# A fused cross-attention block: the read stage's sums moved to TensorE and its steps interleaved with the next block's

## The chip, the cores and the metric

One core of a Trainium2 chip. The metric is the device time of the whole kernel in microseconds, here the median of three runs of the same program; a profiled execution of its own gives the trace. Five engines work side by side and meet only through semaphores: TensorE (PE, matmuls; its weight loads are PEld), VectorE (DVE), ScalarE (ACT), GpSimd (POOL) and SyncE (SP), which here issues most DMAs.

## The reference

Two sequences of 1024 tokens with 2048 features each (512 features x 4 channels). What matters here is the first part:

```
x  = layernorm(x)                                  # over all 2048
y  = einsum('blhc,hoc->bloh', x, W)                # channel sums: 4 channels to 1, for o = Q, K, V
yn = (y - mean(y)) * rsqrt(var(y) + eps) * gamma + beta     # over 512 features, per output
q, k, v = yn[o] @ qkv_w[o].T                       # three 512 x 512 projections
q, k = rope(q), rope(k)
```

After it come causal attention with 16 heads of 32, a gated state write, a second read with two outputs, a large product with the context, a second write, a layer norm and a product with a 2048 x 2048 matrix of signs. None of these is touched.

## The kernel before

Features stand on the partitions and tokens along the free dimension. The work is cut into blocks of T = 512 tokens (NB = 4). Each stage is one function with one instruction list per engine, which its engine runs strictly in order; the order is written out by hand and the waits are semaphore waits.

`setup_phase` (lines 68 to 191) loads the projection weights and constants on SP's queue, and the first two blocks of x on POOL's (line 96), splits the weights into a high and a low part, and makes the rope tables. Its end is a barrier of all engines.

`read_phase` (lines 194 to 517) is the stage changed. X has shape [128, 2 halves, 16 feature tiles, 512]: tile c*4 + a holds channel c of features a*128 to a*128+127. For each block:

- Mean of x: 16 fp32 matmuls with a full 128x128 matrix of 1/2048 (`x_mean`, line 278), so that the sum stands on all partitions; one VectorE pass centres the block (line 428); ScalarE squares it in four pieces (364); 16 more matmuls (`x_var`, 287); ScalarE makes rstd by Ln and Exp (368, 370); one VectorE pass scales (433).
- Channel sums, on VectorE (`read`, 448 and 450): for each output and each of four 128-feature groups one multiplication and three multiply-adds over 512 elements.
- Per output: mean of y (`y_mean`, 301, 4 fp32 matmuls), centring (459), squares, variance (`y_var`, 311), scaling (463), and the affine with gamma and beta on VectorE (466). ScalarE makes ZH, a rounded copy (395), VectorE ZL, the rest (474).
- `project` (327): for each 128-token tile 12 matmuls (ZH x high, ZL x high, ZH x low, for four feature groups) into one PSUM bank, 48 per output. VectorE applies rope to Q and K tiles (486 to 492), ScalarE copies V tiles (415), SP stores them.

The order on PE within a block is: y_mean of all three outputs, with the next block's x_mean between them; y_var of all three; projection of output 0; the next block's x_var; projections of outputs 1 and 2. On VectorE: all channel sums, all centring, x_centre of the next block, scaling, rope of output 0, x_scale of the next block, rope of output 1. There is one ZH and one ZL, so each projection ends before the next output's ZH is made. X of block n+2 is loaded when block n's channel sums are done (249). The normalised x is stored by SP (259) and read again two stages later.

Of the kernel before, what the change touches and what calls it, by code (L numbers as in the profile page):

```python
# [5 lines left out]
F32 = mybir.dt.float32  # L6
# [6 lines left out]
P = 128  # L13
# [52 lines left out]

def setup_phase(nc, io, t):

    with ExitStack() as ctx:
        def ev(name, **k):  # L70
# [10 lines left out]
        idf = t["ident"]  # L81
# [7 lines left out]
                 (idf[:], io["ident"]), (t["masks"][:], io["masks"]), (t["read1"][:], io["read1"]),  # L89
                 (t["read1_gb"][:], io["read1_gb"])]  # L90
        with nc.Block() as block:
            @block.gpsimd
            def _(eng):
                eng.wait_ge(w_loaded.sem, w_loaded.at())
                for half in range(2):
                    eng.dma_start(t["X"][:, half], io["x"][:, :, half * T:(half + 1) * T]).then_inc(t["x_in"][half].sem, t["x_in"][half].unit)
# [10 lines left out]
            def _(eng):  # L107
# [56 lines left out]
                eng.wait_ge(dve_order.sem, dve_order.next(0))  # L164
                eng.wait_ge(w_loaded.sem, w_loaded.at())
# [5 lines left out]
            def _(eng):  # L171
# [18 lines left out]
                eng.activation(t["masks_r"][:], t["masks"][:], ACT.Copy).then_inc(act_order.sem, 1)  # L190
# [3 lines left out]
def read_phase(nc, io, t):  # L194

    with ExitStack() as ctx:
# [7 lines left out]
        SQ = sb("SQ", [P, 2, HC, T])  # L206
# [4 lines left out]
        RT = sb("RT", [P, 2, H])  # L211
        OUT = sb("OUT", [P, TT, H])
        ps = ctx.enter_context(nc.psum_tensor("ps1", [P, 8, 512], F32))
        MEAN, VAR, YM, YV, PJ = 0, 1, (2, 3, 1), (2, 3, 2), 4

        x_in = t["x_in"]
        xn_out = [ev(f"xn_out{a}", unit=16) for a in range(2)]
        mean, cent, xn, rsx = ev("mean"), ev("cent"), ev("xn"), ev("rsx")

        sq, sq_used = ev("sq", per=7, credit=4), ev("sq_used", per=7, credit=4)  # L220
        y, rs = ev("y", per=3), ev("rs", per=3)
        ym, yc, z, zh, zl = (ev(n, per=3) for n in ("ym", "yc", "z", "zh", "zl"))
        pj = ev("pj", per=3 * TT, credit=1)
        pjq_used = ev("pjq_used", per=2 * TT)
        pjv_used = ev("pjv_used", per=TT, credit=TT)
        qk_ready = ev("qk_ready", per=2 * TT)
        stored = [ev(f"stored{tt}", per=3, unit=16, credit=16) for tt in range(TT)]
        assert L // T == 2

        def blocks(eng, body):  # L230

            with eng.Fori(0, B - 1) as b:
                for half in range(2):
                    body(b * 2 + half, half, b, True)
            for half in range(2):
                body(NB - 2 + half, half, B - 1, half == 0)

        def slot(half, k):

            return (half + k + 1) % 2  # L240

        with nc.Block() as block:
            @block.gpsimd
            def _(eng):
                with eng.Fori(0, B - 1) as b:
                    for half in range(2):
                        eng.wait_ge(xn_out[half].sem, xn_out[half].at(b))
                        eng.wait_ge(y.sem, y.at(b * 2 + half, 3))
                        eng.dma_start(X[:, half], io["x"][:, :, bass.ds((b * 2 + half + 2) * T, T)]).then_inc(x_in[half].sem, x_in[half].unit)

            @block.sync
            def _(eng):
                for tt in range(TT):
                    eng.sem_inc(stored[tt].sem, 16)
                with eng.Fori(0, B) as b:
                    for half in range(2):
                        i = b * 2 + half
                        eng.wait_ge(xn.sem, xn.at(i))
                        eng.dma_start(io["xn"][:, :, bass.ds(i * T, T)], X[:, half]).then_inc(xn_out[half].sem, xn_out[half].unit)
                        for o in range(3):  # L260
                            for tt in range(TT):
                                if o < 2:
                                    eng.wait_ge(qk_ready.sem, qk_ready.at(i, o * TT + tt + 1))
                                else:
                                    eng.wait_ge(pjv_used.sem, pjv_used.at(i, tt + 1))
                                eng.dma_start(
                                    io["qkv_s"][:, o, bass.ds(b * (NH // 2), NH // 2), half * TT + tt:half * TT + tt + 1, :],
                                    OUT[:, tt].rearrange("p (h a d) -> p h a d", h=NH // 2, a=1)).then_inc(stored[tt].sem, stored[tt].unit)
                for half in range(2):
                    eng.wait_ge(xn_out[half].sem, xn_out[half].at(B - 1))  # L270
                for tt in range(TT):
                    eng.wait_ge(stored[tt].sem, stored[tt].at(NB - 1, 3))

            @block.tensor
            def _(eng):
                def x_mean(half, first, last):
                    for f in range(first, last):
                        mm = eng.matmul(ps[:, MEAN], t["ones_d"][:], X[:, half, f], start=f == 0, stop=f == NF - 1,
                                        skip_group_check=True)
                    return mm  # L280

                def x_var(i, k0, slot_of):

                    for g in range(4):
                        eng.wait_ge(sq.sem, sq.at(i, k0 + g + 1))
                        for f in range(HC):
                            mm = eng.matmul(ps[:, VAR], t["ones_d"][:], SQ[:, slot_of(g), f],
                                            start=g + f == 0, stop=g + f == 6)
                        mm.then_inc(sq_used.sem, sq_used.unit)

                eng.wait_ge(x_in[0].sem, x_in[0].at())
                x_mean(0, 0, NF).then_inc(mean.sem, mean.unit)
                x_var(0, -4, lambda g: g % 2)

                def body(i, half, b, more):
                    def y_mean(o):
                        eng.wait_ge(y.sem, y.at(i, o + 1))
                        if o == 2:
                            eng.wait_ge(rsx.sem, rsx.at(i))
                        for hc in range(HC):  # L300
                            mm = eng.matmul(ps[:, YM[o]], t["ones_h"][:], Y[:, o, hc], start=hc == 0, stop=hc == HC - 1,
                                            skip_group_check=True)
                        mm.then_inc(ym.sem, ym.unit)

                    def y_var(o):
                        eng.wait_ge(sq.sem, sq.at(i, o + 1))
                        eng.wait_ge(yc.sem, yc.at(i, o + 1))
                        if o == 2:
                            eng.wait_ge(rs.sem, rs.at(i, 1))
                        for hc in range(HC):  # L310
                            mm = eng.matmul(ps[:, YV[o]], t["ones_h"][:], SQ[:, slot(half, o + 1), hc],
                                            start=hc == 0, stop=hc == HC - 1)
                        mm.then_inc(sq_used.sem, sq_used.unit)

                    def project(o):
                        eng.wait_ge(zh.sem, zh.at(i, o + 1))
                        eng.wait_ge(zl.sem, zl.at(i, o + 1))
                        for tt in range(TT):
                            n = o * TT + tt
                            if o == 0:  # L320
                                eng.wait_ge(pjv_used.sem, pjv_used.at(i, n + 1 - TT))
                            else:
                                eng.wait_ge(pjq_used.sem, pjq_used.at(i, n + 1 - TT))
                            step = 0
                            for ic in range(HC):
                                for zz, ww in ((ZH, "qkv_h"), (ZL, "qkv_h"), (ZH, "qkv_l")):
                                    mm = eng.matmul(ps[:, PJ + tt], zz[:, ic, tt * P:(tt + 1) * P],  # L327
                                                    t[ww][:, bass.ts(o * HC + ic, H)],
                                                    start=step == 0, stop=step == 3 * HC - 1)
                                    step += 1  # L330
                            mm.then_inc(pj.sem, pj.unit)

                    y_mean(0)
                    if more:
                        eng.wait_ge(x_in[1 - half].sem, x_in[1 - half].at(b + half))
                        eng.wait_ge(cent.sem, cent.at(i))
                        x_mean(1 - half, 0, NF // 2)
                    y_mean(1)
                    if more:
                        x_mean(1 - half, NF // 2, NF).then_inc(mean.sem, mean.unit)  # L340
                    y_mean(2)
# [1694 lines left out]
```

## Time and profile before

| | us |
|---|---|
| median of three runs | 2495.5 (2489.01 to 2499.91) |
| profiled execution | 2484.01 |
| its span in the trace | 2482.2 |
| setup stage | 0 to 37.1 |
| read stage | 37.1 to 515.9 |
| TensorE busy over the whole span | 2128.8 (86%) |
| VectorE busy | 1549.5 (62%) |
| ScalarE busy | 905.0 (36%) |

The shares are averages over four stages with different limits; for this change only the first 516 us are to be read, and there stage by stage. A matmul's record includes its way through the array, so the distance between two starts, and not its duration, is what one costs in a sequence. An fp32 matmul with 128x128 or 128x32 weights has two records in the trace.

### The profile page before, as it was taken

How to read it: one execution, taken by the hardware profiler on the slowest of the kernel's cores; microseconds unless marked ns; L12 is line 12 of the kernel's file. 1: busy time of each engine (PE TensorE's matmuls, PEld its weight loads, DVE VectorE, ACT ScalarE, POOL GpSimd, SP SyncE). 2: the span in 40 equal slices, each digit the busy share in tenths (PEclk: the TensorE clock that was granted, in tenths of full speed). 3: DMA queues.
4: the chain of work that ended last, by engine and by line, in shares of the span. 5: the costliest groups of instructions: out<-in, count | busy, mean ns of one | idle time of the engine just before them, and what ended most of it. 6: DMA issues, size and time to landing. Idle time of an engine off the chain costs nothing.

```text
span 2482.2 us, 24495 instructions
## 1 busy us (share of the span) xinstructions
PE 2128.8 (86%) x9202; PEld 1461.8 (59%) x9202; DVE 1549.5 (62%) x1761; ACT 905.0 (36%) x1243; POOL 404.3 (16%) x310
## 2 busy tenths in 40 slices
PE   2688887759999999644799999999999999999998
PEld 1254544445555555323586677766777767766776
DVE  3679788566676777348585484674763855748310
ACT  2132221226777777531532524303433025250200
POOL 0000000054555555200000000111000110001011
PEclk9799888869999999877999999999999999999999
DMA  5125224066666666424264566586565875768676
GB/s 190 71 81 170 47 72 119 17 196 222 225 218 219 218 218 210 145 113 173 97 252 166 227 250 240 156 264 211 212 237 182 234 212 210 280 213 245 159 176 140
DMA packets 179782, 452.09 MB, mean 182 GB/s; under 512 B 63830, under 2 KB 64086, under 8 KB 164558
## 3 DMA queue, kind: packets, MB, share of 16 engines
q1 hardware_dynamic: 145374, 310.90, 36.9%
q0 software_dynamic: 32560, 129.41, 17.2%
q10 hardware_dynamic: 1728, 10.18, 1.2%
q8 instruction: 75, 1.23, 0.2%
q14 instruction: 45, 0.37, 0.1%
HBM read 303.27 MB, written 147.16 MB: 181 GB/s over the span
## 4 chain that ended last, share of the span: by engine, by line
PE 45%; DMA 5%; DVE 4%; ACT 2%; issue 1%; POOL 0%; SPq 0%; POOLq 0%; DVEq 0%; ACTq 0%
PE ps L1499 16%; PE ps L1312 8%; PE ps L1313 8%; PE ps L1314 8%; DMA sign_h<-sign_h_scratch 3%; PE ps L1331 3%; PE ps L1370 1%; DMA up<-up_s_scratch 1%; PE ps L1379 1%; PE ps L1420 1%; DVE Y L1802 1%; ACT L1528 1%; PE ps L1408 1%; DMA wall_a<-wall_s_scratch 1%; ACT E_mlp L1551 0%
## 5 line engine op out<-in xcount | busy, mean ns | idle before, releaser
L1499 PE MATMUL ps<-XH,sign_h 128*128 128x512 f32 x768 | 313.6, 408 | 12.6 <-DMA sign_h<-sign_h_scratch 12.5
L1499 PE MATMUL ps<-XL,sign_h 128*128 128x512 f32 x768 | 300.1, 391 | 0.0
L886 DVE TENSOR_REDUCE maxes<-ps 128x1 f32<-128x512 f32 (+3 forms) x384 | 208.3, 555 | 116.1 <-PE ps L726 84.4
L1312 PE MATMUL ps<-ZH,up 128*128 128x512 f32 x512 | 217.8, 425 | 10.9 <-DVE ZL L1827 8.9
L1313 PE MATMUL ps<-ZL,up 128*128 128x512 f32 x512 | 201.1, 393 | 0.0
L1314 PE MATMUL ps<-ZH,up 128*128 128x512 f32 x512 | 200.7, 392 | 0.0
L819 ACT ACTIVATE probs<-ps 128x512 f32<-128x512 f32 (+3 forms) x384 | 167.5, 485 | 39.9 <-PE ps L751 25.3
L1499 PEld LDWEIGHTS ps<-XH,sign_h 128*128 128x128 f32 x768 | 144.7, 188 | 62.1 <-issue 17.8
L767 PE MATMUL ps<-probs,v_ones 128*64 128x512 f32 (+3 forms) x768 | 171.0, 525 | 0.0
L723 PE MATMUL ps<-turned_k,turned_q 96*128 96x512 f32 (+3 forms) x384 | 159.2, 428 | 12.0 <-DVE maxes L886 10.6
L1499 PEld LDWEIGHTS ps<-XL,sign_h 128*128 128x128 f32 x768 | 144.9, 189 | 34.9 <-issue 6.2
L723 PEld LDWEIGHTS ps<-turned_k,turned_q 96*128 96x128 f32 x384 | 75.7, 198 | 125.2 <-DVE maxes L886 77.4
L327 PE MATMUL ps<-qkv_h,ZH 128*128 128x512 f32 x192 | 84.6, 441 | 61.2 <-issue 32.5
L1312 PE MATMUL ps<-inner_h,proj 128*128 128x512 f32 (+1 forms) x320 | 133.0, 416 | 4.0 <-DVE inner_l L1877 4.0
L751 PE MATMUL ps<-turned_q,turned_k 97*128 97x512 f32 (+3 forms) x384 | 127.8, 388 | 1.8 <-ACT probs L819 1.7
L1224 POOL DMA_DIRECT2D out<-product_scaled x64 | 55.8, 872 | 450.7 <-DVE product_scaled L1892 443.8
L1313 PE MATMUL ps<-inner_l,proj 128*128 128x512 f32 (+1 forms) x320 | 126.9, 396 | 0.0
L1314 PE MATMUL ps<-inner_h,proj 128*128 128x512 f32 (+1 forms) x320 | 126.3, 395 | 0.0
L1312 PEld LDWEIGHTS ps<-ZH,up 128*128 128x128 f32 x512 | 97.0, 189 | 48.9 <-issue 26.4
L1331 PE MATMUL ps<-small,expand_sb 120*128 120x512 f32 x176 | 91.4, 616 | 34.9 <-DVE E_mlp L1727 11.5
L1874 DVE TENSOR_TENSOR product<-ps,silu 128x512 f32<-128x512 f32 x64 | 44.2, 691 | 120.4 <-PE ps L1314 120.3
L1313 PEld LDWEIGHTS ps<-ZL,up 128*128 128x128 f32 x512 | 97.1, 190 | 27.7 <-issue 9.2
(289 smaller groups left out, 4384.0 us busy)
## 6 DMA issues: line engine op xcount, KB each, us to landing
sign_h<-sign_h_scratch SPq DMA_DIRECT2D x256, 256.0 KB, 3.9
up<-up_s_scratch SPq DMA_DIRECT2D x58, 1024.0 KB, 6.3
proj<-proj_s_scratch SPq DMA_DIRECT2D x58, 632.0 KB, 4.0
X<-in_x POOLq DMA_DIRECT2D x4, 4096.0 KB, 14.6
xn_scratch<-X SPq DMA_DIRECT2D x4, 4096.0 KB, 13.7
sign_raw<-in_sign SPq DMA_DIRECT2D x32, 512.0 KB, 7.9
sign_h_scratch<-sign_high SPq DMA_DIRECT2D x32, 512.0 KB, 3.7
sign_l_scratch<-sign_low SPq DMA_DIRECT2D x32, 512.0 KB, 5.2
```

Of the source, the lines that this page charges most:

```text
L327: mm = eng.matmul(ps[:, PJ + tt], zz[:, ic, tt * P:(tt + 1) * P], t[ww][:, bass.ts(o * HC + ic, H)], start=step == 0, stop=step == 3 * HC - 1)
L723: mm = eng.matmul(ps[:, bank, 0:w], ST[0][n % 3][e][0:STACK, q * P:(q + 1) * P], ST[1][n % 3][e][0:STACK, k0:k0 + w], start=True, stop=not ...
L751: mm = eng.matmul(ps[:, SC + e, 0:w], ST[1][v % 3][e][:, k * P:(k + 1) * P], ST[0][v % 3][e][:, q0:q0 + w], start=True, stop=not diag, ski ...
L767: mm = eng.matmul(ps[64 * e:64 * e + 2 * HD, O[h], c:c + w], VO[v % 2][:, k, e], PT[p % NPT][:, e, 0:w], start=k == 0, stop=p + 1 == last_ ...
L819: eng.activation(PT[p % NPT][:, e, 0:w], ps[:, SC + e, 0:w], ACT.Exp, scale=HD ** -0.5).then_inc(ex.sem, ex.unit)
L886: eng.tensor_reduce(MAXES[:, e, q, k0 // T:k0 // T + 1], ps[:, MX[m % 2], 0:w], AX.X, ALU.max).then_inc(mx_read.sem, mx_read.unit)
L1224: eng.dma_start(io["out"][:, m, tokens(u)], RES[a][:], accum_op=ALU.add).then_inc(out[a].sem, out[a].unit)
L1312: eng.matmul(out_ap, lh, rh, start=start, stop=False, skip_group_check=True)
L1313: eng.matmul(out_ap, lh, rl, start=False, stop=False, skip_group_check=True)
L1314: return eng.matmul(out_ap, ll, rh, start=False, stop=stop, skip_group_check=True)
L1331: eng.matmul(ps[:, banks[n % len(banks)]], EX[:, e], SM[:], start=True, stop=True).then_inc(xp.sem, xp.unit)
L1499: mm = eng.matmul(ps[:, sign_bank(m)], s[q][:, f], x[:, n], start=n + w == 0, stop=n == NF - 1 and w == len(operands) - 1, skip_group_chec ...
```

## The change

Four things are changed, all in the setup and read stages.

1. Layout of X. A tile now holds 32 features x 4 channels: channel c stands on partitions 32c to 32c+31. So x is loaded, and its normalised form stored, by four DMAs of 32 partitions and 1 MB each. The scratch tensor for it has its feature tiles outermost.
2. Channel sums on TensorE: a block matrix of 128x32 for each tile and output sums the four channels of 32 features; four such matmuls write the four quarters of a PSUM bank. ScalarE copies the bank to Y. There are two banks for it. The matrices are 768 KB, loaded in the setup stage.
3. All feature sums in quarters: tile j's sum goes to partitions 32j to 32j+31, with 128x32 weights; ScalarE copies the bank, and one full matmul with ones adds the quarters and spreads the result. The affine moves from VectorE to ScalarE. The passes over X on VectorE are cut in four pieces.
4. The order: period n does the projections of block n-1 between the read of block n and the mean and variance of block n+1. The outputs go V, Q, K (`OUTPUT = (2, 0, 1)`); the projections have three PSUM banks instead of four.

```diff
+def rows_of_x(t, x_c, c, n):
+    q = P // C
+    return (t["X"][c * q:(c + 1) * q, n % 2], x_c[c][:, :, n * T:(n + 1) * T])
...
-                    eng.dma_start(t["X"][:, half], io["x"][:, :, half * T:(half + 1) * T])...
+                    for c in range(C):
+                        eng.dma_start(*rows_of_x(t, io["x_c"], c, half))...
...
+        PJ, RD, XS, YM, YV = (0, 1, 2), (3, 4), 5, 6, 7
+        OUTPUT = (2, 0, 1)
...
+                for n in range(2, NB):                                  # POOL
+                    half = n % 2
+                    eng.wait_ge(xn_out[half].sem, xn_out[half].at(n // 2 - 1, C))
+                    eng.wait_ge(rd.sem, rd.at(n - 2, 3 * HC))
+                    for c in range(C):
+                        eng.dma_start(*rows_of_x(t, io["x_c"], c, n))...
...
+                def quarters(bank, weights, tiles, start, stop):        # PE
+                    for j in range(4):
+                        mm = eng.matmul(ps[j * (P // 4):(j + 1) * (P // 4), bank], weights(j), tiles[:, j], start=start, stop=stop, ...)
+                def close(bank, k, done):
+                    eng.matmul(ps[:, bank], t["ones_h"][:], R[:, k], start=True, stop=True)...
+                def x_var(n, g):
+                    eng.wait_ge(x_act.sem, x_act.at(n, X_SQUARED + g))
+                    if g == 0:
+                        eng.wait_ge(xn.sem, xn.at(n, HC))               # all four x_centre
+                    quarters(XS, lambda j: t["ones_p"][:], SQX[g % 2], ...)
+                def read(n, s):
+                    for hc in range(HC):
+                        eng.wait_ge(xn.sem, xn.at(n, X_SCALED + hc + 1))
+                        past(eng, y_in, n, s * HC + hc - 1)             # ACT's copy of two sets before
+                        quarters(RD[hc % 2], lambda j: t["read1"][:, 4 * hc + j, OUTPUT[s]], X[:, n % 2, 4 * hc:4 * hc + 4], ...)
```

The order of the steps in period n (old is block n-1, now is n, new is n+1; PE, then ScalarE, then VectorE), as the new lists have it:

```
PE:  project(old,0) y_var(old,2) read(now,0) y_var_close(old,2) x_mean(new) y_mean(now,0) x_mean_close(new)
     y_mean_close(now,0) | project(old,1) read(now,1) y_var(now,0) y_mean(now,1) y_var_close(now,0)
     x_var(new,0..1) y_mean_close(now,1) | project(old,2) read(now,2) x_var(new,2..3) y_var(now,1)
     y_mean(now,2) x_var_close(new) y_var_close(now,1) y_mean_close(now,2)
ACT: v_out(old,0) y_square(old,2) v_out(old,1) affine(old,1) v_out(old,2..3) y_var_copy(old,2) take_y(now,0)
     z_high(old,1) y_rstd(old,2) x_copy(new) y_mean_copy(now,0) affine(old,2) y_square(now,0) x_square(new,0..1)
     take_y(now,1) z_high(old,2) y_var_copy(now,0) y_mean_copy(now,1) y_rstd(now,0) x_square(new,2..3)
     y_square(now,1) affine(now,0) take_y(now,2) z_high(now,0) x_copy(new) y_var_copy(now,1)
     y_mean_copy(now,2) x_rstd(new) y_rstd(now,1)
DVE: scale(old,1) x_scale(now,0..3) z_low(old,1) centre(now,0) scale(old,2) x_centre(new,0) rope(old,1,0)
     x_centre(new,1) rope(old,1,1) x_centre(new,2) z_low(old,2) x_centre(new,3) rope(old,1,2) rope(old,1,3)
     centre(now,1) scale(now,0) rope(old,2,0..3) z_low(now,0) centre(now,2)
```

The second argument of a step is the output in the new order (0 is V, 1 is Q, 2 is K), or the piece of X. `project` waits for z_high and z_low of its output, z_high for the end of the projection before, and `take_y` is the four copies out of the read banks. SP stores V of the old block, then the normalised x of the current one, then Q and K of the old one.

## Rows read from the trace of the kernel before

**Rows 1.** Stretches of the read stage: start:end, length; busy us (instructions); clock; DMA.
```profile
37.00:90.70 53.70, 32.71 (x64) 13.81 (x64) 17.39 (x3) 10.13 (x7) 0.00 (x0) 0.80 0.00 0
...
197.30:303.00 105.70, 87.41 (x258) 51.53 (x257) 88.87 (x104) 26.45 (x22) 1.15 (x1) 0.90 0.35 110
...
409.00:511.00 102.00, 71.38 (x217) 46.21 (x217) 71.75 (x102) 18.78 (x18) 0.00 (x0) 0.83 0.28 80
```
**Rows 2.** VectorE: groups by line of 0:620, rope in order of time, the longest wait.
```profile
L450 DVE SCALAR_TENSOR_TENSOR Y<-X,read,Y 128x512 f32<-128x512 f32 x144 | 98.6, 747 | 1.3
L463 DVE TENSOR_TENSOR Y<-Y,R 128x2048 f32<-128x2048 f32 x12 | 27.4, 2286 | 4.4 <-ACT R L370 4.4
L466 DVE TENSOR_SCALAR Y<-Y,read_gb 128x512 f32<-128x512 f32 x48 | 23.0, 543 | 0.4
L448 DVE TENSOR_SCALAR Y<-X,read 128x512 f32<-128x512 f32 x48 | 20.1, 482 | 0.4 <-DVE OUT L492 0.2
...
165.82 0.69 DVE L492 TENSOR_TENSOR OUT<-RT 128x512 f32<-128x512 f32 x1
...
167.93 0.69 DVE L492 TENSOR_TENSOR OUT<-RT 128x512 f32<-128x512 f32 x1
...
DVE ZL L474 <- ACT ZH L395: 11.5, 3, 6.7
```
**Rows 3.** TensorE in order of time: start, length, line, how many records.
```profile
199.72 0.39 PE L327 MATMUL ps<-qkv_h,ZH 128*128 128x512 f32 x1
...
203.57 0.39 PE L327 MATMUL ps<-qkv_l,ZH 128*128 128x512 f32 x1
...
207.56 5.40 PE L301 MATMUL ps<-Y,ones_h 128*128 128x512 f32 x8 [3.60 <-DVE Y L450]
212.80 7.03 PE L278 MATMUL ps<-X,ones_d 128*128 128x512 f32 x16
```
**Rows 4.** TensorE in order of time, quarters in the block stage.
```profile
1449.67 0.39 PE L1314 MATMUL ps<-ZH,up 128*128 128x512 f32 x1
1449.99 1.06 PE L1408 MATMUL ps<-x,ones_p 128*32 128x512 f32 x8
1450.98 0.50 PE L1312 MATMUL ps<-ZH,up 128*128 128x512 f32 x1
1451.32 0.39 PE L1313 MATMUL ps<-ZL,up 128*128 128x512 f32 x1
```
**Rows 5.** ScalarE: two squares in order of time, then groups by line.
```profile
250.49 3.70 ACT L364 ACTIVATE SQ<-X 128x2048 f32<-128x2048 f32 x2
...
L368 ACT ACTIVATE R<-ps,eps 128x512 f32<-128x512 f32 x16 | 10.9, 684 | 29.7 <-PE ps L287 19.6 <-PE ps L311 10.0
L370 ACT ACTIVATE R<-R 128x512 f32<-128x512 f32 x16 | 10.1, 630 | 0.5
L415 ACT ACTIVATE OUT<-ps 128x512 f32<-128x512 f32 x16 | 9.6, 599 | 60.7 <-PE ps L327 60.7
```
**Rows 6.** The setup stage's end: POOL's drain (duration ns, start us), PE's first matmul.
```profile
L91 POOLq DRAIN  x1: 25138/25138/25138, 11.7 to 11.7; - x1
...
37.10 16.27 PE L278 MATMUL ps<-X,ones_d 128*128 128x512 f32 x32 [37.10 <-PEq L91]
```
**Rows 7.** DMA queues of three windows, 121:136, 1021.5:1025 and 512.9:515.9.
```profile
q0 software_dynamic: 1040, 4.19, 76.0%
...
q1 hardware_dynamic: 96, 0.26, 30.2%
...
q1 hardware_dynamic: 1040, 0.26, 38.4%
```
**Rows 8.** TensorE after an idle time, as in Rows 1.
```profile
244.00:253.00 9.00, 0.05 (x1) 0.03 (x1) 6.99 (x8) 5.64 (x5) 0.00 (x0) 0.64 0.00 0
253.00:256.80 3.80, 3.79 (x9) 3.06 (x10) 3.76 (x5) 1.19 (x1) 0.00 (x0) 0.50 0.00 0
```
**Rows 9.** SP's queue in order of time, the attention stage's first load.
```profile
515.94 0.36 SPq L593 DMA_DIRECT2D Gq<-qkv_scratch  x1
```

More of the change, by code:

```diff
@@ L230, in blocks @@
[L230 to L240, printed above, removed]
+        xn_out = [ev(f"xn_out{a}", per=C, unit=16) for a in range(2)]
+        xm, xv = ev("xm", per=2), ev("xv", per=HC + 1)
+        x_act = ev("x_mean_copied_squares_variance_copied_rstd", per=HC + 3)
@@ L275, in _ @@
             def _(eng):
-                def x_mean(half, first, last):
-                    for f in range(first, last):
-                        mm = eng.matmul(ps[:, MEAN], t["ones_d"][:], X[:, half, f], start=f == 0, stop=f == NF - 1,
+                def quarters(bank, weights, tiles, start, stop):
+                    for j in range(4):
+                        mm = eng.matmul(ps[j * (P // 4):(j + 1) * (P // 4), bank], weights(j), tiles[:, j], start=start, stop=stop,
                                         skip_group_check=True)
@@ L280, in x_mean @@
                     return mm
[L282 to L341, printed above, removed]
-                    y_var(0)
-                    y_var(1)
-                    y_var(2)
-                    project(0)
-                    if more:
-                        eng.wait_ge(yc.sem, yc.at(i, 3))
-                        x_var(i, 3, lambda g: slot(half, 4 + g))
-                    project(1)
-                    project(2)
@@ L352, in _, with x_mean @@
-                blocks(eng, body)
+                def close(bank, k, done):
+                    eng.matmul(ps[:, bank], t["ones_h"][:], R[:, k], start=True, stop=True).then_inc(done.sem, done.unit)
+                def x_mean(n):
+                    eng.wait_ge(x_in[n % 2].sem, x_in[n % 2].at(n // 2, C))
+                    past(eng, x_act, n - 1, X_RSTD)
+                    for g in range(HC):
+                        mm = quarters(XS, lambda j: t["ones_p"][:], X[:, n % 2, 4 * g:4 * g + 4], g == 0, g == HC - 1)
+                    mm.then_inc(xm.sem, xm.unit)
@@ L366, in rstd @@
-                def rstd(k, bank, order, i, done):
-                    eng.activation(R[:, k], ps[:, bank], ACT.Ln, bias=t["eps"][:]).then_inc(order.sem, 1)
-                    eng.wait_ge(order.sem, order.next(i))
-                    eng.activation(R[:, k], R[:, k], ACT.Exp, scale=-0.5).then_inc(done.sem, done.unit)
-                def x_rstd(n, i, k):
-                    eng.wait_ge(sq_used.sem, sq_used.at(i, k))
-                    x_chain.start()
-                    rstd(0, VAR, x_chain, n, rsx)
-                    x_chain.close()
@@ new lines, in y_rstd, with affine @@
+                def y_rstd(n, s):
+                    eng.wait_ge(yv.sem, yv.at(n, 2 * s + 2))
+                    rstd(1 + OUTPUT[s], YV, y_act)
+                def affine(n, s):
+                    o = OUTPUT[s]
+                    eng.wait_ge(ys.sem, ys.at(n, s + 1))
+                    for hc in range(HC):
+                        ins = eng.activation(Y[:, o, hc], Y[:, o, hc], ACT.Identity, bias=gb[:, 1, o, hc:hc + 1], scale=gb[:, 0, o, hc:hc + 1])
+                    ins.then_inc(z.sem, z.unit)
@@ L1952, in build @@
                 t["X"] = sbf("X", [P, 2, NF, T])
-                t["x_in"] = [Count(first, nc, f"x_in{half}", unit=16) for half in range(2)]
+                t["x_in"] = [Count(first, nc, f"x_in{half}", per=C, unit=16) for half in range(2)]
                 setup_phase(nc, io, t)
```

496 lines of the change are left out of this document (327 added, 169 removed).

## The prediction

> **What bounds the kernel now.** I read the stretches of the stage first, then the costliest groups by line, the waits of one block, and the order of time around single steps. The read stage runs from 37.1 us (first matmul) to 515.9 us (first load of the attention stage): 478.8 us of the 2482.2 [rows 6, 9]. The 37 us ahead of it are loads and constants. Then comes a start of 53.7 us in which mean, centring, squares, variance and scaling of the first block stand one behind the other (PE busy 32.7, DVE 17.4), and then four blocks of some 106 us each; the last has no next block to prepare. In a full block DVE is busy 88.9 of 105.7 us and PE 87.4 at a granted clock of 0.90, so neither is hidden by the other: they take turns [rows 1]. VectorE's waits show where: 11.5 us per block are ZL waiting for ZH, which waits for the projection before it [rows 2]. So there are two things to gain: less work on both engines, and fewer turns.
>
> **The work removed and added, for one block.**
> VectorE: the channel sums are 16 instructions for each of three outputs: 98.6/4 + 20.1/4 = 29.7 us. The affine is 23.0/4 = 5.8 us. Both leave it, nothing comes: 88.9 - 35.5 = 53.4 us [rows 1, 2].
> TensorE: one projection matmul follows the last in (203.57 - 199.72)/17 = 0.227 us, so one output (48) takes 10.9 and three 32.7. A full fp32 matmul is two records; 16 records take 7.03, less the tail of the last, so 0.86 for a matmul [rows 3]. Mean and variance are now 16+16+12+12 = 56 of them: 48 us. They become quarters. The trace has this operation in the block stage: four 128x32 quarters (8 records) take 1.06 us, and the matmul behind starts 0.99 after the first [rows 4]. They run beside each other, as one full matmul would. The bounds for a set of four are 0.86 (a full matmul) and 1.19 (from where the next would have started, 1449.90, to where the pace is back, 1451.09). I take 1.0, since sets stand in runs of one to six. New per block: 8 sets for x, 6 for y, 12 for the channel sums = 26 us, and 8 closing matmuls of 0.86 = 6.9. Sum: 32.7 + 26 + 6.9 = 65.6 us.
> ScalarE has 26.5 us per block now [rows 1]. Added: 12 copies out of PSUM, 5 copies of partial sums, 12 affine pieces. A copy has 0.60 us, Exp from SBUF to SBUF 0.63, some 0.5 when they follow closely [rows 5]. 29 x 0.5 to 0.6 = 16: 43 us.
> So TensorE, at 65.6, becomes the bound, and the order decides what comes on top.
>
> The Trainium skill (TensorEngine Tiling, Key Properties) says that a change of tiling mode drains TensorE, which speaks against putting quarters between full matmuls. Here the two changes around a single set cost 1.19 - 0.86 = 0.33 us [rows 4]; with five such runs per block that is 1.7 us, and 26 x 0.86 + 1.7 = 24.1 against the 26 I use.
>
> **One block of the pipeline, walked.** Time 0 is the start of project(n-1, first output). A full DVE pass over 2048 elements is 2.2 us, a rope tile 2.1, an ACT pass over 2048 1.85, Ln and Exp 1.35 [rows 2, 5].
> - PE projects V to 10.9. DVE ends centre of the last output at 2.5, scale at 4.7, the four x_scale at 7.0, 9.2, 11.4, 13.7: under the projection. y_var to 11.9, four read sets to 15.9, a close, x_mean(n+1) to 20.8, y_mean 21.8, two closes to 23.6. ACT, behind its four copies, makes z_high of Q at 18.6; z_low is done at 21.0. That wait is hidden.
> - project Q 23.6 to 34.5. Under it on DVE: centre (26.0), scale (28.2), x_centre, rope, x_centre, rope, x_centre to 39.1. Read sets of the second output: the third needs ACT's first copy, and ACT is busy with x_square until 36.8, so they end at 39.4, not 38.5. y_var, y_mean to 41.4; the variance copy stands behind z_high(K) (42.1), close to 43.6: PE idle 1.3.
> - x_var(n+1) waits for the fourth x_centre. It stands on DVE behind z_low(K), which waits for z_high at 42.1: z_low 44.4, x_centre 46.7. PE is idle from 43.6 to 46.8. This is the place of the pipeline that is late.
> - x_var 2 sets, a close: 49.7. project K to 60.6. DVE: two ropes, centre, scale, and four ropes of K at 57.5 to 63.9, with the matmuls. The three PSUM banks just do: the fourth K tile starts at 57.9, its bank is read at 57.5.
> - read sets 60.6 to 64.6, x_var, y_var, y_mean to 68.6, closes to 71.2. z_low of V is there at 69.6. The next block starts at 71.2.
> PE waits 5.6 us of it: 71.2 = 65.6 + 5.6.
>
> **Clock.** After 3.6 us of idle 8 records took 5.40 us where 16 take 7.03 at the full rate [rows 3], and after an idle stretch of 9.0 the granted clock was 0.50 for 3.8 us [rows 8]: about 1.9 us lost each time. The 3.2 us gap of the walk may or may not do this; I take 2 us per block: 73.2. Five lost us per block are the upper end.
>
> **Start and end.** Start: x_mean in 4 sets, partly at half rate, 6.7; copy and close 8.3; four x_centre to 17.4; x_var cold and chained with the squares to 24.5; copy, close, Ln, Exp 27.5; x_scale to 36.4 where 53.7 stands now. Block 0 alone (no projection) by the same walk: its DVE does centre and four x_centre before ACT's second square at 52.8, and its three outputs go one behind the other: PE ends at 77, with one cold start 80 us after the stage starts. End: project V 10.9, wait for z_low 17.0, project Q 27.9, z_high and z_low 32.3, project K 43.2, rope 45.5, store 2.6, two cold starts: 52.
>
> **Transfers of x.** X now goes in and out as four 1 MB transfers of 32 partitions. Over all 128, packets of 4 KB take 0.760 x 16 x 15 us/1040 = 175 ns. The trace has transfers from 32 partitions: the attention output, 64 packets of 4 KB in 0.302 x 16 x 3.5 us = 16.9 us: 264 ns each, 1.5 times as long [rows 7]. The bounds are 1.0 (several queued transfers may fill the paths) and 2.0; I take 1.5, the row. The Trainium skill (SBUF — State Buffer, Door 1: The DMA port swizzle) has the rule: 32 partitions reach 8 of 16 ports, and two transfers on different partitions don't add up. By it the rate would be 218 GB/s, an estimate of 38.5 us for the first 8.4 MB where the row gives 37; the trace agrees in direction.
> This is paid ahead of the stage: POOL's drain, and with it every engine's first instruction, lasts until both halves of X have landed (11.7 + 25.1 = 36.8) [rows 6]. 24.6 us of traffic become 37: +12.4; the block matrices are 768 KB instead of 24 KB, 2 us at the 8.4 MB/24.6 us of now. Setup ends at 51.5 instead of 37.1: +14.4. Nothing hides it.
> In the loop, X(n+2) is issued at 64.6 and takes 1.5 + 13.3 x 1.5 = 21.5 us, and beside it run eight stores of OUT, each 0.384 x 16 x 3 us/16 = 1.15 us of all engines, half of which fall in: landed at 91, or 20 in the next block, where x_mean wants it at 16.8. 3.5 us late, for two blocks: +7. The xn store (13.7 to 35) is in nobody's way: Q's store stands behind it on SP, but OUT is not written again before 55. POOL issues four transfers per block, and nothing is queued behind them.
>
> **Sum.** Setup 51.5 + start and block 0 80 + three blocks 3 x 73.2 = 219.6 + late X 7 + end 52 = 410. Now: 515.9. So -106 us. The profiled execution took 2484.0 (span 2482.2): 2378. The median of the three timed runs is 11.5 above it, so **2390 us**. The later stages compute the same from the same tiles; xn_scratch lies in another order, but is still read in 2 KB pieces.
>
> **Rivals.**
> - Faster (0.13): the 32-partition transfers run at the full rate (-12.4 - 7) and sets go at 0.86: 4 x 26 x 0.14 = -14.6. With the forecast's rest: 2356. For it: the bounds of rows 4 and 7; against: both rows lie nearer the value I took.
> - The engines still take turns (0.17): two banks for the channel sums make every PE set wait for ACT's copy, which itself stands behind squares and affines. Then each of 12 sets costs 0.8 more, 9.6 per block, 4 x 9.6 = +38: 2428. For it: ACT's long in-order list. Against: ACT has 43 us of work in 73.
> - The change doesn't do what it says (0.05): projections don't fall between the next block's steps, since a late z_low holds up everything behind it on PE, and the block stays at 105.7 less about the removed DVE work, 88: 4 x 15 = +60: 2450.
> - Slower (0.03): quarters run side by side only with the same weights (ones), and the channel sums, each with its own block matrix, go one after another: 4 x 0.86 - 1.0 = 2.44 us more for 48 sets = +117: 2507. It decides from 2.2 us more per set (106/48). Against: in [rows 4] each quarter of ones loads its weights too.
> The forecast itself has 0.62, with 2365 to 2415 of its own. Range 2350 to 2436. A measurement of this kernel can tell some 0.5% (12.5 us) from no change. Chances: faster 0.95, same 0.02, slower 0.03.
>
> **What would show it.** Setup: POOL's drain ends near 51 us; at 39 the transfer step is wrong. Block period, from one first x_scale to the next: 73 to 77; DVE busy about 53 of it and PE about 66 to 70. Four quarters of the channel sums: 1.0 us per set; 3.4 would be the slower rival. The longest PE wait inside a block is x_var for x_centre, some 3 us, and x_mean(2) and x_mean(3) wait for the transfer. Granted clock 0.93 or more. If instead the read sets wait for ACT's copies each time, the second rival is the case. The attention stage and the rest should take 1966 us as before; if they don't, the sum is wrong where I did not look.

## The result, and the profile after

| kernel | median us | fastest to slowest | ratio to before (95%) |
|---|---|---|---|
| before | 2495.83 | 2489.01 to 2499.91 | 1 |
| after | 2365.15 | 2360.09 to 2370.22 | 0.9482 [0.9461, 0.9503] |

The forecast was 2390 with a range of 2350 to 2436. The profiled execution took 2370.22 us (before: 2484.01), its span in the trace is 2368.3 (2482.2): the spans differ by 113.9 us, the medians by 130.7.

The page of the kernel after, span and busy times:
```profile
span 2368.3 us, 25199 instructions
PE 2051.8 (87%) x9650; PEld 1401.6 (59%) x9650; DVE 1409.7 (60%) x1546; ACT 981.7 (41%) x1371; POOL 409.8 (17%) x322
```
Stretches of the read stage after, to be held against [rows 1]: setup, start, block 0, blocks 1 and 2, then block 3 with the end. Columns as there: start:end, length, busy us of PE, PEld, DVE, ACT, POOL, granted clock, DMA share, GB/s.
```profile
0.00:56.00 56.00, 0.00 (x0) 0.00 (x0) 14.46 (x27) 12.52 (x12) 5.81 (x12) 1.00 0.95 224
56.00:83.80 27.80, 15.00 (x68) 3.21 (x68) 8.88 (x4) 11.30 (x9) 0.00 (x0) 0.82 0.00 0
83.80:141.10 57.30, 40.40 (x235) 12.80 (x235) 31.14 (x14) 32.12 (x39) 2.58 (x4) 0.82 0.48 104
141.10:217.50 76.40, 68.46 (x370) 36.54 (x368) 53.94 (x50) 45.53 (x55) 2.58 (x4) 0.93 0.70 152
217.50:290.20 72.70, 65.94 (x370) 36.00 (x369) 54.01 (x50) 45.59 (x55) 0.00 (x0) 0.98 0.62 136
290.20:400.00 109.80, 90.65 (x435) 58.45 (x433) 68.32 (x81) 49.59 (x63) 0.00 (x0) 0.95 0.40 96
```
PE now fills 65.94 of 72.70 us of a block where it filled 87.41 of 105.70, and DVE 54.01 instead of 88.87.

The end of setup and the first load of the attention stage, which answer to [rows 6, 9]:
```profile
L98 POOLq DRAIN  x1: 41779/41779/41779, 14.4 to 14.4; - x1
...
400.41 0.34 SPq L702 DMA_DIRECT2D Gq<-qkv_scratch  x1
```
The drain lasts 41.8 us instead of 25.1 and ends at 56.2. From there to 400.41 are 344 us, where 37.1 to 515.94 were 479.

Groups by line of the read stage after (read sets, affine, copies of read sets; x, busy us, mean ns, idle before):
```profile
L289 PE MATMUL ps<-X,read 128*32 128x512 f32 x384 | 52.1, 663 | 19.5 <-ACT Y L445 14.9 <-DVE X L549 4.6
L468 ACT ACTIVATE Y<-Y,read_gb 128x512 f32<-128x512 f32 x48 | 35.2, 804 | 21.8 <-DVE Y L559 21.8
L445 ACT ACTIVATE Y<-ps 128x512 f32<-128x512 f32 x48 | 28.1, 594 | 37.2 <-PE ps L289 37.2
```
The 14.9 us in the first of these rows are waits of the channel sums for ScalarE's copy. Nearly all of them stand in block 0, which has no projection to fill them:
```profile
109.37 3.64 PE L289 MATMUL ps<-X,read 128*32 128x512 f32 x16 [7.44 <-ACT Y L445]
...
126.95 3.53 PE L289 MATMUL ps<-X,read 128*32 128x512 f32 x16 [6.26 <-ACT Y L445]
```
TensorE in blocks 1 and 2 after, in order of time: x_mean of block 1, then the rows of block 2 with the waits that are read below, and its longest runs of quarters (8 records are a set of four):
```profile
156.38 5.34 PE L289 MATMUL ps<-X,ones_p 128*32 128x512 f32 x32 [3.13 <-DMA X<-in_x]
...
224.82 3.77 PE L289 MATMUL ps<-X,read 128*32 128x512 f32 x32
...
231.58 3.64 PE L289 MATMUL ps<-X,ones_p 128*32 128x512 f32 x32 [1.93 <-DMA X<-in_x]
...
251.52 1.93 PE L289 MATMUL ps<-X,read 128*32 128x512 f32 x16 [0.61 <-ACT Y L445]
...
260.57 3.28 PE L289 MATMUL ps<-SQX,ones_p 128*32 128x512 f32 x16 [3.00 <-DVE X L543]
```
VectorE after, the scaling of X, whose distances are the block periods (57.3, 76.4, 72.7), and TensorE's first matmuls of V's projection in the last two periods (blocks 2 and 3 of x), whose distance is block 3's:
```profile
83.85 8.90 DVE L549 TENSOR_TENSOR X<-X,R 128x2048 f32<-128x2048 f32 x4 [10.29 <-ACT R L422]
...
141.13 8.89 DVE L549 TENSOR_TENSOR X<-X,R 128x2048 f32<-128x2048 f32 x4
...
217.56 8.89 DVE L549 TENSOR_TENSOR X<-X,R 128x2048 f32<-128x2048 f32 x4
...
290.21 8.89 DVE L549 TENSOR_TENSOR X<-X,R 128x2048 f32<-128x2048 f32 x4
```
```profile
285.20 0.79 PE L358 MATMUL ps<-qkv_h,ZH 128*128 128x512 f32 x1
...
347.53 0.47 PE L358 MATMUL ps<-qkv_h,ZH 128*128 128x512 f32 x1
```

### The profile page after: what moved, and what is told of

It is laid out like the page before. It is cut to its first block, busy times and chain, and to the rows that moved or that the text cites. A ratio compares the mean times of both kernels' runs of the same rounds, so it can differ in the third digit from the quotient of the medians.

```text
span 2368.3 us, 25199 instructions
## 1 busy us (share of the span) xinstructions
PE 2051.8 (87%) x9650; PEld 1401.6 (59%) x9650; DVE 1409.7 (60%) x1546; ACT 981.7 (41%) x1371; POOL 409.8 (17%) x322
## 4 chain that ended last, share of the span: by engine, by line
PE 48%; DVE 5%; DMA 4%; ACT 2%; issue 1%; POOL 0%; POOLq 0%; SPq 0%; DVEq 0%; ACTq 0%
PE ps L1608 17%; PE ps L1421 8%; PE ps L1422 8%; PE ps L1423 8%; PE ps L1440 3%; DMA sign_h<-sign_h_scratch 2%; PE ps L1479 1%; PE ps L1488 1%; DMA up<-up_s_scratch 1%; DVE Y L1911 1%; PE ps L1529 1%; ACT L1637 1%; PE ps L1517 1%; DMA wall_a<-wall_s_scratch 1%; ACT E_mlp L1660 0%
## 5 line engine op out<-in xcount | busy, mean ns | idle before, releaser
L1440 PE MATMUL ps<-small,expand_sb 120*128 120x512 f32 x176 | 91.8, 619 | 34.9 <-DVE E_mlp L1836 11.5
L1788 ACT ACTIVATE silu<-ps 128x512 f32<-128x512 f32 x64 | 38.3, 599 | 194.3 <-PE ps L1423 194.0
```

What stands on the lines that cost most here:

```text
L1440: eng.matmul(ps[:, banks[n % len(banks)]], EX[:, e], SM[:], start=True, stop=True).then_inc(xp.sem, xp.unit)
```

## The experiments

All times of the read stage end at the first load of Gq; after's is 400.41.

**How well a trace repeats.** Both kernels were run again unchanged.

> The kernel before, unchanged, for a second profile. The profiled execution of before (2484.0 us) lies 12 us under the median of its runs and that of after (2370.2) 5 above, so the traces show 114 us of gain and the medians 131. Theory: the rest lies behind the read stage, in stages that the change does not touch: a second profile has the same read stage (37.1 to 515.9, within 2 us) and another length behind it (1966 us then, up to 1985 now). Rival: the read stage itself varies by ten us from run to run, by the phase of TensorE's clock.

> The kernel before, a third profile: read stage over at 515.9 to 517.2 us again; the rest 1966 to 1986 us if it is chance, over 1974 if the first profile was the exception.

> The changed kernel once more, for a second profile beside one of before on the same chip. If the 12 us that the medians show beyond the read stage (1974.7 us behind it before, 1962.9 after, by medians less the stage) are chance, its unchanged stages take anything between 1958 and 1986 us, with the difference in the attention stage. If they come with the change (another layout of the stored x, other buffer addresses), they take under 1970 again.

The stage of before ended at 517.12 and 514.41 (first: 515.94), that of after at 397.18 (first: 400.41), with periods of 73.1 and 72.5 where the first trace has 76.4 and 72.7. In block 1 x_mean waited 2.12 us for X in the second trace and its 32 records took 3.64; in the first trace it waited 3.13 and they took 5.34. The time behind the stage was 1985.9 and 1967.9 us for before (first: 1966.3) and 1967.5 for after (first: 1967.9), though the code there is the same. The read stage thus repeats within some 3 us, the rest only within 20; its attention stage alone took 531.9 and 519.5 us in the two repeats of before. So effects in the read stage are read from the stage's end, where they can be told apart to some 3 us, and medians follow as a check. Where a difference from after is given below, the first trace comes first and the second behind it. That one execution of before is 20 us longer in a stage that no edit touches also says how far 113.9 and 130.7 may lie apart; some 10 us of that difference are not settled: the second trace of after showed 1967.5, which fits chance as well as a cause in the change.

**e3: is the late start the drain, or the bytes?** The first eight loads of x go from SP's queue, not POOL's, behind the constants; the later loads get a semaphore of their own, and one semaphore of VectorE's setup list is replaced by another with the same order.
```diff
 # setup, POOL
-    for c in range(C):
-        eng.dma_start(*rows_of_x(t, io["x_c"], c, half)).then_inc(t["x_in"][half].sem, t["x_in"][half].unit)
 # setup, SP, behind the constants
+    for c in range(C):
+        eng.dma_start(*rows_of_x(t, io["x_c"], c, half)).then_inc(t["x_in"][half].sem, t["x_in"][half].unit)
```


> The changed kernel with one edit: the eight loads of the first two blocks of x are issued from SP's queue, behind the constants, and not from POOL's; the loop's two later loads keep POOL and get a semaphore of their own. Theory: the setup stage ends at 56.3 us only because POOL's drain lasts until both halves of x have landed over 32 partitions each; from SP's queue nothing drains, so the barrier falls with VectorE's last instruction near 32 us and the first matmul waits for the first half alone: 11.2 us plus 4.2 MB at the 197 GB/s of the trace plus the block matrices, near 35 us. Expected: first matmul at 33 to 37 us, total 20 us shorter (2345). Rival: the barrier's time is the bytes' own, so it is paid wherever they are issued, and x_mean of block 1 waits instead: less than 5 us shorter.

Median 2346.43 (2344.72 to 2349.97), ratio 0.9419 [0.9377, 0.9461]. POOL's drain, first matmul and end of the stage:
```profile
L97 POOLq DRAIN  x1: 41/41/41, 11.2 to 11.2; - x1
...
35.35 5.61 PE L289 MATMUL ps<-X,ones_p 128*32 128x512 f32 x32 [35.35 <-DMA X<-in_x]
...
374.20 0.33 SPq L705 DMA_DIRECT2D Gq<-qkv_scratch  x1
```
x_mean waits for its data and no longer for the sequencer's barrier: 21.1 us earlier, and the stage ends 26.2 (23.0) earlier. The drain takes 41 ns where it took 41.8 us. The rate of the loads is that of the kernel after, so it is the drain that was paid: block 0 needs 4 MB, POOL's drain waited for 8. DMA of e3 from 12 to 60 us, in 40 slices of 1.2 us:
```profile
GB/s 349 160 205 193 196 198 200 198 196 213 225 198 203 193 196 198 203 193 232 205 198 198 198 198 193 203 205 225 203 200 193 196 198 205 184 80 0 0 0 0
```

**e1: partitions or memory order?** x comes from a second copy in the order of the tile, one 4 MB transfer over 128 partitions per block; the queue stays POOL's.
```diff
-    for c in range(C):
-        eng.dma_start(*rows_of_x(t, io["x_c"], c, half)).then_inc(t["x_in"][half].sem, t["x_in"][half].unit)
+    eng.dma_start(t["X"][:, half], io["x_r"][:, :, half * T:(half + 1) * T]).then_inc(t["x_in"][half].sem, t["x_in"][half].unit)
```


> The changed kernel with x loaded over all 128 partitions at once, one transfer of 4 MB per block from a second copy of x in the order of the tiles; stores and everything else as they are. Theory: the setup stage is 19 us longer than before because each transfer has 32 partitions (197 GB/s in the trace, 390 before): POOL's drain ends near 39 us (36.9 plus 2 for the block matrices), and x_mean of blocks 2 and 3 no longer waits for its transfer (1.5 and 1.9 us now). Total 19 to 21 us shorter than the changed kernel. Rival: the rate is lost to the order of the rows in memory, or to the block matrices beside it, not to the partitions: the drain still ends after 50 us.

One run: 2336.89. The drain is back at before's length, and PE starts behind it:
```profile
L98 POOLq DRAIN  x1: 24933/24933/24933, 11.7 to 11.7; - x1
...
36.96 5.14 PE L287 MATMUL ps<-X,ones_p 128*32 128x512 f32 x32 [36.96 <-PEq L98]
```
The start is 19.5 us earlier and x_mean waits for no transfer in any block. The stage ends at 375.05, 25.4 (22.1) earlier, more than the 19 to 21 expected: the waits for X that go were 3.13 and 1.93 us in the first trace, not 1.5 and 1.9, and the slow records behind the longer one go with it. This copy lies in another order than the x of before and is loaded as fast (24.9 and 25.1 us); what the two share is 128 partitions.

**e2: do two queues on different partition halves add up?** e3, with partitions 64 to 127 loaded from ACT's queue, issued as its first instructions.
```diff
 # SP
-    for c in range(C):
+    for c in range(2):
 # ACT, ahead of all else
+    for c in range(2, C):
+        eng.dma_start(*rows_of_x(t, io["x_c"], c, half)).then_inc(t["x_in"][half].sem, t["x_in"][half].unit)
```


> The kernel with x on SP's queue, but with two of each block's four transfers (partitions 64 to 127) on ScalarE's queue, so that both halves of the partitions are written at once. Theory A (the limit lies with the partitions that are in use at a time): both queues together move about 390 GB/s, the first block has landed by 25 us, the barrier at 32 us is then what the first matmul waits for, and both blocks are in by 36. Theory B (the 16 engines work through one transfer after another whatever the queue): first matmul at 35 us as with SP alone, the second block in at 56.

One run: 2347.13, stage end 385.02. PE started later than in e3, at 43.82, released by the barrier, not by x: ACT's loads were ahead of the constants in time, `read_gb` landed late, and VectorE's setup waited 24.4 us for it. So the expected early start failed. But the rate is plain. DMA of e2 from 24 to 36 us, both queues (packets, MB, share), with the weights landed at 13.5:
```profile
DMA packets 2087, 4.11 MB, mean 342 GB/s; under 512 B 83, under 2 KB 83, under 8 KB 2087
...
q1 hardware_dynamic: 1107, 2.17, 56.4%
q10 hardware_dynamic: 980, 1.94, 48.8%
```
342 GB/s where e3 had 193 to 232 in nearly every slice, and all of x was in by 47 us where e3 needed until 55: transfers on the two halves add when they stand in two queues. The Trainium skill (SBUF — State Buffer, "Can I just issue two DMAs to hit both halves?") says that two concurrent transfers, at partitions 0 and 64, moved only 6% more than a single one; here the measurement differs and decides. Whether the second queue does it by itself is not tested: two queues on the same half were not run.

**e5: is TensorE the bound?** Each set of four channel-sum quarters is issued twice, into the same bank.
```diff
+    quarters(RD[hc % 2], lambda j: t["read1"][:, 4 * hc + j, OUTPUT[s]], X[...], True, True)
```


> The changed kernel with each set of four channel-sum matmuls issued twice into the same bank (same values): 12 more sets per block on TensorE, nothing else. Theory: TensorE is the bound of a middle block, so the added time appears, less what falls into its two waits (3.0 us for the fourth x_centre, 0.6 for the bank copy): 12 x 0.89 - 3.6 = 7 us per block, 25 to 32 us for four blocks (2394). Rival A: VectorE's and ScalarE's chain is the bound: under 8 us. Rival B: sets with different matrices do not run beside each other, 3.4 us each: 160 us.

Median 2403.21 (2396.89 to 2407.43), ratio 0.9641 [0.9594, 0.9687]. Two of its block periods and the stage's end:
```profile
146.82:226.65 79.83, 75.61 (x466) 39.12 (x465) 53.96 (x51) 45.77 (x55) 2.58 (x4) 0.98 0.68 145
226.65:307.49 80.84, 76.62 (x466) 39.46 (x465) 53.96 (x51) 45.77 (x55) 0.00 (x0) 0.96 0.57 123
...
429.20 0.34 SPq L703 DMA_DIRECT2D Gq<-qkv_scratch  x1
```
PE gains 76.62 - 65.94 = 10.7 us per block, 0.89 per set, and the stage 28.8 us (32.0) for 48 sets, 0.60 (0.67) each. The rest fell into waits that were there, though not where it was expected: the wait for the fourth x_centre is still 3.00 us in both blocks, and the one for X is gone. From the fourth x_scale to the end, where PE has no X to wait for, the time rose by 121.7 - 110.2 = 11.5 us, all of the added work. So a cost of PE reaches the end by two thirds or more: PE is the bound, with some room at its waits. That DVE and ACT are not is read from their busy times, 54 and 46 us of 80; no run adds work to them.

**e4: how much is the order alone?** The instructions are after's; only the interleaving goes. Each period runs the steps of the block before first and then those of its own and the next block, on PE, ACT and DVE, and SP stores in that order.
```diff
-for n in range(NB + 1):
-    old, now, new = n > 0, n < NB, n + 1 < NB
+for n, own in [(n, own) for n in range(NB + 1) for own in (False, True)]:
+    old, now, new = n > 0 and not own, n < NB and own, n + 1 < NB and own
```


> The changed kernel with the interleaving undone: in each period all steps of the old block (projections, rope, its last scaling) stand ahead of all steps of the current and next block, on PE, ScalarE and VectorE; SP stores Q and K of the old block before the normalised x. All instructions are kept. Theory: most of the gain is the order. The current block's own chain takes 57 us (block 0 of the changed kernel, first x_scale to next x_scale) and the old block's 46 (the last block's projections); behind one another they give about 103 us per block where 73 to 76 stand now: read stage 430 us instead of 344, total 85 to 90 us longer (2450). Rival: the gain is the work taken off VectorE (35 us per block) and TensorE (22 us), and the order matters little: less than 25 us longer.

Median 2458.5 (2454.19 to 2462.36), ratio 0.9858 [0.9814, 0.9903]. One period and the end:
```profile
185.38:287.56 102.18, 73.78 (x368) 38.48 (x368) 54.23 (x50) 45.82 (x54) 2.58 (x4) 0.88 0.52 113
...
485.56 0.34 SPq L702 DMA_DIRECT2D Gq<-qkv_scratch  x1
```
The stage ends 85.2 us (88.4) later: 102.2 per block against 72.7, with DVE and ACT busy as in after and PE at a clock of 0.88. That is the worth of the interleaving, given the moved work. Against before, e4's stage ends 515.94 - 485.56 = 30.4 us earlier. In this the late start costs 19.6, the way from the first matmul to the end of the first x_scale is 17.5 shorter (36.1 for 53.6), and what follows is 32.5 shorter (392.7 for 425.2). So in a serial order 35.5 us less of DVE work made a full block hardly shorter, 102.2 for 105.7. The work in the order of before was not run: that order already has steps of the next block between its own and is less serial than e4's, so 30 us is the worth of the other three changes in a serial order and not a share of the whole. The changes within them (channel sums on TensorE, quarters for the means, affine on ScalarE) were not tried one by one.

**e6: the longest wait of a block.** x_centre of the last pair of tiles ahead of z_low of K on DVE.
```diff
-if old:
-    z_low(n - 1, 2)
 if new:
     x_centre(n + 1, 3)
 if old:
+    z_low(n - 1, 2)
+if old:
     rope(n - 1, 1, 2)
```


> The changed kernel with one swap on VectorE: the fourth x_centre of the next block ahead of z_low of K, not behind it. Theory: x_var waits 3.0 us for this x_centre in blocks 1 and 2, and VectorE is idle 2.8 us just before, so the wait goes and nothing else is later: 6 us shorter in the two blocks, with the clock perhaps 8 (2358); both periods, first x_scale to first x_scale, 3 us shorter. Rival: the third projection then waits for z_low, which ends at the same time as before, and the gap only moves: less than 2 us.

Its blocks 1 and 2:
```profile
141.00:209.30 68.30, 64.65 (x370) 35.78 (x370) 53.98 (x51) 45.56 (x55) 2.58 (x4) 1.00 0.79 168
209.30:278.00 68.70, 64.48 (x370) 35.67 (x369) 53.85 (x51) 45.41 (x55) 0.00 (x0) 1.00 0.67 146
...
249.71 1.92 PE L289 MATMUL ps<-SQX,ones_p 128*32 128x512 f32 x16
```
The wait of 3.00 is gone, the 16 records behind it take 1.92 instead of 3.28, the clock is 1.00, and the period falls from 76.4 and 72.7 (73.1 and 72.5) to 68.3 and 68.7. For block 2 the wait and the clock are the whole of it: 3.00 + 1.36, less 0.49 of longer waiting for X. Block 1 of the first trace also had the wait of 3.13 for X with 5.34 us of records behind it, which the second trace has without any edit at 2.12 and 3.64; that part is not e6's. The stage ends at 389.87, 10.5 (7.3) earlier. The medians (2359.73, 2349.91 to 2365.72; ratio 0.9482 [0.9439, 0.9524]) cannot tell it from after.

**e7 and e11: the edits together.** e7 is e3 and e6, and ACT's copy of y's variance ahead of z_high of K. e11 is e7 with e1's transfers over 128 partitions.
```diff
 # ACT, e7 and e11
+if now:
+    y_var_copy(n, 0)
 if old:
     z_high(n - 1, 2)
-    y_var_copy(n, 0)
```


> The changed kernel with three edits: x's first loads on SP's queue, the fourth x_centre ahead of z_low of K on VectorE, and on ScalarE the copy of V's variance ahead of z_high of K. Theory: the three lie one behind the other on the path, so they add: 20 us at the start, 10 in the blocks (the 10.5 of the read stage that the second alone gave) and 1.2 for each of two blocks where PE waits for that copy: 31 us, 2334 against 2365. Rival: with the stage starting earlier or its periods shorter, the load of x for blocks 2 and 3 comes later against x_mean (1.9 us of waiting now) and takes the gain of the shorter periods: 24 us or less.

> The kernel with the three edits, and x loaded over all 128 partitions in one transfer per block (from a second copy of x in the order of the tiles) by SP's queue for the first two blocks and by POOL's in the loop. Theory: the first half of x is in before VectorE's last setup instruction, so the first matmul falls with the barrier near 33 us (35.4 now), and both waits of x_mean for its transfer go (2.1 and 3.15 us) with the half-rate stretch behind the second (1.7): 9 us, read stage over at 362 instead of 371, total 2329 against 2338. Rival: the waits are for the row of stores and the order on the queues, not for the rate; they stay, and the gain is 3 us or less.

e7: median 2337.77 (2333.78 to 2341.18), ratio 0.938 [0.9361, 0.9399], stage end 371.20: 27.4 less in medians and 29.2 (26.0) in the stage where 31 was expected. Its periods are 69.0 and 71.7. In the second of them x_mean waits longer for X:
```profile
202.83 5.34 PE L289 MATMUL ps<-X,ones_p 128*32 128x512 f32 x32 [3.15 <-DMA X<-in_x]
```
It waits 3.15 where after waited 1.93 in this block, and the 32 records behind take 5.34 instead of 3.64. The rival names this wait, but e7 does not show that the shorter period makes it: after's own block 1 had 3.13 and 5.34, and e6, with the shorter periods, waited 1.86 and 2.42 with 3.64 behind. The third edit shows no gain: PE's 1.22 us for that copy are gone, and K's projection waits 1.34 us for a rope instead, which it did not in these blocks of after or e6.
e11: median 2332.85 (2327.72 to 2343.01), ratio 0.937 [0.9343, 0.9397], with periods of 66.8 and 66.8, and
```profile
32.01 4.93 PE L287 MATMUL ps<-X,ones_p 128*32 128x512 f32 x32 [32.01 <-PEq L97]
...
362.56 0.34 SPq L704 DMA_DIRECT2D Gq<-qkv_scratch  x1
```
x_mean waits for X no more. The stage ends 8.6 us before e7's and 37.8 (34.6) before after's. It has the lowest median of all, faster than before and than after, though its interval overlaps e7's.

## Why the prediction was right

It was right in sign and in mechanism, and the time lies in its range: 2365.15 in 2350 to 2436, 25 us under the 2390, at the lower edge of the 2365 to 2415 that the forecast gave itself. It is nearer to the 2356 of the faster rival, but neither of that rival's two reasons held: the loads ran 1.8 times as long and not at the full rate, and a set cost 0.89 (e5) to 0.94 and not 0.86. By its steps:

- **TensorE becomes the bound at 65.6 us per block**: measured 65.94, of which 1.4 are the half rate behind x_centre; e6, at a clock of 1.00, shows 64.5. e5 shows that what is added there reaches the end, by two thirds or more. A run of 32 records takes 3.77, 0.94 per set, where 1.0 was used. The slower rival, quarters with different matrices one after another, would have shown 13.8 for that run.
- **VectorE 53.4, ScalarE 43**: 54.0 and 45.6. The affine on ScalarE takes 804 ns per piece (35.2/48 = 733 as they follow closely) where 500 to 600 were taken, and the sum has 5 copies of partial sums where the list has 8, two of x and six of y. The sum of neither engine's work decides; VectorE's order does, at one place.
- **The walk of the block**: x_var waits for the fourth x_centre 3.00 (3.2 in the walk), the third read set for ACT's copy 0.61 (0.9). Period 73.2 plus 3.5 of late X: 76.4 and 72.7 here, 73.1 and 72.5 in the second trace. X was late by 3.13 and 1.93 (2.12 and 1.67), where 3.5 were taken each time. The clock lost behind x_centre was 3.28 - 1.92 = 1.4 us in block 2 and 1.7 in block 1, where 2 were taken; another 5.34 - 3.64 = 1.7 behind the longer wait for X were not in the sum. e6 confirms place and price of the wait for x_centre. The wait for the variance copy was 1.22 (1.3).
- **The rival that engines still take turns** is out for the full blocks: it needed 0.8 us for each of 12 sets, 9.6 per block, and such a block has one wait of 0.61. Block 0 does have such waits, 7.44 and 6.26; the 80 us forecast for the start and this block, whose outputs "go one behind the other", held them.
- **The rival that the change doesn't interleave**: no projection of blocks 1 and 2 waits for z_low in the trace. e4 made a serial order by hand, which is another cause with the same effect: the stage ends 85 us later, more than the 60 that the rival was priced at.
- **Start**: 27.4 us from the first matmul to the first x_scale (27.5), and 84.7 us from the first matmul to the second x_scale (80 + 4.7).
- **Setup, a term sized wrong.** 51.5 was forecast, 56.46 came. The step took 1.5 for 32 partitions from [rows 7], whose row is a lone attention output. The queue's row for 16 to 56 us after is
```profile
q0 software_dynamic: 2000, 7.67, 98.7%
```
0.987 x 16 x 40 us / 2000 = 316 ns per packet against the 175 of before: 1.8, near the upper bound of 2.0. The Trainium skill (SBUF — State Buffer, Door 1: The DMA port swizzle) gives some 218 GB/s for 32 partitions where the transfer is large; the 193 to 232 of e3's slices lie around it, most of them some 10% below. That the drain holds every engine until both halves have landed was read rightly; e3 and e1 take that 20 us away in two ways.
- **Block 3, the largest error.** The sum has "three blocks 3 x 73.2". The last of them prepares no next block: 8 sets and 2 closing matmuls (9.7 us) and the wait for x_centre with its clock are not there. From one V projection to the next are 347.53 - 285.20 = 62.3 us, 56.3 of them busy: the sum had 10.9 too much. The text itself says of the kernel before that the last block has no next to prepare, and then left it out of its own sum.
- **End**: 400.41 - 347.53 = 52.9, forecast 52.
- **The sum**: stage end 400.4 for 410. Setup +5.0, start and block 0 nothing, blocks 1 and 2 -4.4 (76.7 each forecast, 149.1 measured for both), block 3 -10.9, end +0.9: -9.4 of the -9.6. Up to the fourth x_scale, forecast and measurement stand at 289.6 and 290.2, since the late setup and the short blocks cancel: the agreement there is partly luck.
- **The rest of the kernel**: forecast 1966 behind the stage, measured 1967.9.

Of the 25 us between 2390 and 2365, then, 8 lie in the trace: 2378 was forecast for the profiled execution, which took 2370.2. The other 17 come from the step to the median: the 11.5 of before was added, but after's profiled execution happened to be the longest of its four, 5 above their median. That part is chance.

## What to carry to other kernels

When two engines take turns, taking work from one gains little until the order lets them run side by side: here 35.5 us less of VectorE's work shortened a block by 3.5 us in a serial order, and the interleaved order then by another 29. In a pipeline price first and last periods by themselves, by striking what each of them does not do. Before you split a load over fewer partitions, look at who drains its queue: eight loads on another queue were worth 19 us of median. Before you credit an edit with a shorter wait, look at the same wait in a second trace of the unchanged kernel: the one for X was 3.13 us in one and 2.12 in the other.

## What the runs showed of the hardware

- The drain at the end of the setup stage waits for loads still outstanding on POOL's own queue (41.8 us, and 24.9 with transfers over 128 partitions), and the barrier with it; with the same loads on SP's queue the drain took 41 ns and the first matmul came at 35.35 instead of 56.46.
- Loads to 32 partitions ran at 193 to 232 GB/s from one queue and at a mean of 342 from two queues on different halves (e2; two queues on one half were not run).
- A scaling with bias on ScalarE from SBUF to SBUF takes 804 ns for 128x512, a copy out of PSUM 594.
- After 3.00 us of idle, 16 records of quarters took 3.28 us in one block and 3.64 in the other, at a granted clock of 0.58 and 0.50; without the idle 1.92, at 1.00 (e6). After 3.13 (after) and 3.15 us (e7), 32 records took 5.34 at 0.68; after 1.93 (after) and 2.42 us (e6), 3.64 at 1.00. So the time after the idle was paid at the lower level of 1.2 GHz, in whole or in part.
- The stages that no edit touched took 1958 to 1986 us in the traces of all these kernels.
